# Two layers of local attention and gated feed-forward in one block instead of four, with the two sequences of a pair staggered

## The reference

```python
x = x + _layernorm(_L1_attn_ref(_layernorm(x, axis=-1), ...), axis=-1)
x = x + _layernorm(_L1_ffn_ref(_layernorm(x, axis=-1), L1_ffn_wqkv, ..., L1_ffn_w2, L1_ffn_b2), axis=-1)
x = x + _layernorm(_L2_attn_ref(_layernorm(x, axis=-1), ...), axis=-1)
```

```python
def _layer(x, wqkv, qs, ksc, wo, lg, lb, w1, b1, w2, b2):
    b, n, _ = x.shape
    h = shift_token(x)
    qkv = h @ wqkv
    q, k, v = jnp.split(qkv, 3, axis=-1)
    ...
    q = l2norm(q) * qs
    k = l2norm(k) * ksc
    q, k = rotary_xpos(q, k)
    o = local_attention(q, k, v)
    o = o.transpose(0, 2, 1, 3).reshape(b, n, INNER)
    x = x + o @ wo
    h = shift_token(x)
    mu = h.mean(-1, keepdims=True)
    var = h.var(-1, keepdims=True)
    h = (h - mu) / jnp.sqrt(var + 1e-05) * lg + lb
    h = h @ w1 + b1
    a, g = jnp.split(h, 2, axis=-1)
    h = a * jax.nn.gelu(g, approximate=False)
    x = x + h @ w2 + b2
    return x
```

## Time and profile before

| | us |
|---|---|
| median of three runs (3698.55 to 3700.59) | 3698.94 |
| span of the profiled execution, first to last instruction | 3714.3 |
| busy in it: PE, DVE, ACT, POOL | 2972.4, 2362.2, 1568.7, 773.5 |
| first call of `l1_ffn`: attention, layer 1 | 109.04 |
| feed-forward, layer 1 | 32.95 |
| attention, layer 2 | 106.73 |
| feed-forward, layer 2, and the stage's normalisation | 37.90 |

### The profile page before, as it was taken

The page is one execution under the profiler, slowest core; times in us unless marked ns, Lnnn a source line. Parts: engine busy times, 40 slices in busy tenths (PEclk is TensorE's granted clock), DMA queues, the critical chain, the costliest instruction groups (busy, mean ns, idle before and its releaser), DMA issues. The chain is left out here.

```text
span 3714.3 us, 89913 instructions
## 1 busy us (share of the span) xinstructions
PE 2972.4 (80%) x35888; PEld 2017.2 (54%) x35888; DVE 2362.2 (64%) x6687; ACT 1568.7 (42%) x3160; POOL 773.5 (21%) x823
## 2 busy tenths in 40 slices
PE   3768888689876788868986778876998688798996
PEld 2635556556554455556654445655655354475654
DVE  7575755665777466566677646646667776565457
ACT  4144534434344453534443544353444354344432
POOL 4121312121113121222111322132111122112101
PEclk8679999689987899969998889986999798999998
DMA  1011100000001100000000110000010101000000
GB/s 41 1 36 33 23 7 3 2 2 19 18 1 46 34 19 7 3 2 3 23 14 1 52 31 16 8 2 1 4 31 6 33 21 37 7 3 3 20 18 7
DMA packets 64209, 59.21 MB, mean 16 GB/s; under 512 B 16371, under 2 KB 53156, under 8 KB 63782
## 3 DMA queue, kind: packets, MB, share of 16 engines
q1 hardware_dynamic: 62550, 52.72, 5.2%
q10 hardware_dynamic: 1232, 0.61, 0.1%
HBM read 35.76 MB, written 2.10 MB: 10 GB/s over the span
## 5 line engine op out<-in xcount | busy, mean ns | idle before, releaser
L1333 POOL TENSOR_TENSOR l1t_ss<-l1t_ss,neghalf 128x16 f32<-128x16 f32 x48 | 182.4, 3799 | 333.2 <-DVE l1t_ss L1367 333.2
L256 ACT ACT_TABLE_LOAD x64 | 82.1, 1283 | 304.7 <-PEq L1677 106.5
L2260 ACT ACTIVATE l2r_P<-l2r_bank_score 128x512 f32<-128x512 f32 x240 | 130.3, 594 | 137.2 <-PE l2r_bank_score L1982 137.2
L2260 ACT ACTIVATE l2a_P<-l2a_bank_score 128x512 f32<-128x512 f32 x240 | 130.3, 594 | 131.5 <-PE l2a_bank_score L1982 131.5
L1544 PE MATMUL l1t_ring<-l1f_qkv,x_normT 128*128 128x512 f32 x288 | 162.5, 693 | 12.2 <-ACT x_normT L1238 12.2
L191 POOL TENSOR_TENSOR ln_y_rstd<-ln_var_eps,neghalf 128x4 f32<-128x4 f32 x52 | 52.8, 1015 | 546.5 <-DVE ln_var_eps L212 510.6
L2152 DVE CUSTOM_DVE_ANT_0 l2r_masked<-l2r_bank_ring,l2r_neg_wide 128x512 bf16<-128x512 f32 (+1 forms) x192 | 111.5, 622 | 57.5 <-PE l2r_bank_ring L1951 57.2
L2152 DVE CUSTOM_DVE_ANT_0 l2a_masked<-l2a_bank_ring,l2a_neg_wide 128x512 bf16<-128x512 f32 (+1 forms) x192 | 111.7, 622 | 56.0 <-PE l2a_bank_ring L1951 55.1
L1951 PE MATMUL l2r_bank_ring<-l2r_k_head,l2r_q_head 32*128 32x128 f32 x1824 | 131.6, 285 | 14.9 <-DVE l2r_m L2152 7.4
L1982 PE MATMUL l2a_bank_score<-l2a_q_head,l2a_k_head 32*128 32x128 f32 x1920 | 141.8, 285 | 1.8 <-DMA l2a_q_head<-l2a_shiftT 0.8
L1951 PE MATMUL l2a_bank_ring<-l2a_k_head,l2a_q_head 32*128 32x128 f32 x1824 | 133.1, 287 | 12.2 <-DVE l2a_m L2152 5.3
(11 more groups left out here) (1197 smaller groups left out, 8454.5 us busy)
## 6 DMA issues: line engine op xcount, KB each, us to landing
l1t_v_low<-l1t_v SPq DMA_DIRECT2D x84, 130.0 KB, 2.3
l2x_w<-in_L_ffn_w SPq DMA_DIRECT2D x72, 128.0 KB, 2.3
l1f_qkv<-in_L_ffn_wqkv SPq DMA_DIRECT2D x6, 768.0 KB, 4.3
l1t_v_low_last<-l1t_v_last SPq DMA_DIRECT2D x28, 130.0 KB, 2.3
l1f_tables<-in_l_tables SPq DMA_DIRECT2D x6, 512.0 KB, 5.7
l2e_w_last<-in_L_ffn_w SPq DMA_DIRECT2D x24, 128.0 KB, 2.2
x_in<-in_L_attn_hidden_states SPq DMA_DIRECT2D x8, 256.0 KB, 3.0
out<-x_res SPq DMA_DIRECT2D x8, 256.0 KB, 2.6
```

Of the source, the lines that this page charges most:

```text
L256: act.activation(b.warm[:, column:column + 1], b.neghalf[:, 0:1], func)
L1333: pool.tensor_tensor(ss[:, n % 2], ss[:, n % 2], b.neghalf[:, 0:2 * H8], ALU.pow).then_inc(s["rn_ready"], 1)
L2260: act.activation(self.P[:, use % self.P_RING].rearrange("k h q -> k (h q)"), self.score_bank(h, g)[:, :], ACT.Exp, scale=self.scale).then_ ...
```

## The change

The four blocks of a call become one, with one set of semaphores and one ring for everything.

- `TILE_ORDER` puts the first sequence's tiles ahead: (0,0), (1,0), (0,1), (2,0), (3,0), (1,1), (2,1), (3,1), written (tile, sequence). The first sequence's rows are complete after the fifth tile, the second's after the eighth.
- The parts of the feed-forward become functions of one sequence: `turn_rows`, `turn_shifted`, `turn_normed`, `up`, `down` on PE; `shifted_stats`, `shifted_norm`, `gate`, `add_rows` on DVE; `turned_rows`, `turned_normed`, `gate` on ACT. The streams are written out with these between the attention's last tiles and layer 2's first.
- The bias `b2` becomes row 85 of the third slice of `w2`, and row 85 of the third slice of `hid` holds ones; the product with a row of ones goes.
- Layer 2's tables, `qkv`, `wo` and feed-forward weights are loaded as soon as layer 1 has read its own, between the transfers of `v_low` in SP's stream.

```diff
-        for d in range(DEPTH):
-            before = l1_ffn_attention(nc, b, w, lw, d, before)
-            before = l1_ffn_mlp(nc, b, f, lw, d, before)
-    return before
...
+BIAS_CHUNK, BIAS_ROW = len(HID_ROWS) - 1, HID_ROWS[-1][1]
+HID_K = [rows + (i == BIAS_CHUNK) for i, (c, rows) in enumerate(HID_ROWS)]
+TILE_ORDER = [(0, 0), (1, 0), (0, 1), (2, 0), (3, 0), (1, 1), (2, 1), (3, 1)]
+TL = len(TILE_ORDER)
+LAST_FIRST = TILE_ORDER.index((NT - 1, 0))
```

SP's stream:

```diff
+            lw.load_tables(sync, 0, s["tab_in"])
+            lw.load_qkv(sync, 0, s["qkv_in"])
+            lw.load_wo(sync, 0, s["wo_in"])
+            lw.load_mlp(sync, 0, s["mlp_in"])
+            sync.wait_ge(s["tables_ready"], 1)
+            lw.load_tables(sync, 1, s["tab_in"])
+            for n, (d, j, p) in enumerate(tiles):
+                if n == TL:
+                    sync.wait_ge(s["v_psum"], TL)
+                    lw.load_qkv(sync, 1, s["qkv_in"])
+                    sync.wait_ge(s["tile_psum"], TL)
+                    lw.load_wo(sync, 1, s["wo_in"])
+                if n == TL + 2:
+                    sync.wait_ge(s["fy_psum"], PAIR)
+                    lw.load_mlp(sync, 1, s["mlp_in"])
                 sync.wait_ge(s["v_ready"], n + 1)
```

The last product, old and new, and the order of PE's stream (`a` is the feed-forward part, `n` the tile, `i` the tile's place in its layer):

```diff
-                    pe.matmul(out, b.ones[0:1, :], lw.b2[:], start=True, stop=False)
...
+                for j in range(NT):
+                    for i, rows in enumerate(HID_K):
+                        last = pe.matmul(bank[:, j * D:(j + 1) * D], hid[0:rows, p, i, j * 128:(j + 1) * 128],
+                                         lw.w2[0:rows, i, :], start=i == 0, stop=i == parts - 1)
+                last.then_inc(s["fy_psum"], 1)
...
+                    if i == LAST_FIRST + 2:
+                        turn_rows(a)
+                    values(n)
...
+                    if i == LAST_FIRST + 2:
+                        turn_shifted(a)
+                    if i + 1 < TL:
+                        turn_shift(n + 1)
+                n = here + TL - 1
+                turn_normed(a)
+                turn_output(n)
+                up(a, 0)
+                output(n)
+                up(a, 1)
+                turn_rows(a + 1)
+                up(a, 2)
+                turn_shifted(a + 1)
+                down(a)
+                turn_normed(a + 1)
...
+            tile_steps(0)
+            turn_x(2)
+            up(1, 0)
+            project(TL, "qk")
+            up(1, 1)
+            project(TL, "v")
+            up(1, 2)
+            project(TL + 1)
+            down(1)
+            turn_qk(TL)
+            turn_x(3)
+            maxima(TL)
+            project(TL + 2)
+            scores(TL)
+            turn_shift(TL)
+            tile_steps(TL)
+            for i in range(parts):
+                up(3, i)
+            down(3)
```

ACT's stream between the layers, and DVE's at the end of the call:

```diff
+            tile_steps(0)
+            warm(act, b, ACT.Gelu)
+            turned_normed(0)
+            turned_output(TL - 1)
+            gate(0, 0)
+            gate(0, 1)
+            turned_rows(1)
+            gate(0, 2)
+            turned_normed(1)
+            turned_x(2)
+            gate(1, 0)
+            copy_qk(TL)
+            gate(1, 1)
+            square_and_v(TL)
+            gate(1, 2)
+            copy_qk(TL + 1)
+            square_and_v(TL + 1)
+            warm(act, b, ACT.Exp, 1)
+            turned_qk(TL)
+            turned_x(3)
...
+            add_rows(2)
+            result_stats(0)
+            gate(3, 0)
+            gate(3, 1)
+            gate(3, 2)
+            dve.wait_ge(b.x_stored, 16 * PAIR)
+            result_add(0)
+            add_rows(3)
+            result_stats(1)
+            result_add(1)
```

More of the change, by code:

```diff
@@ L1282, in l1_ffn_attention @@
         place = {taker: i for i, taker in enumerate(takers)}
         def v_low_done(n):
[L1285 removed]
+            return sum(16 + 16 * (j > 0) for d, j, p in tiles[0:n + 1])
         def bank_of(what, n):
@@ L1538, in take, with turn_x, project @@
                 return bank_of(what, n)
-            def project(n, parts="qkv"):
-                j, p = tiles[n]
-                for what in parts:
+            def turn_x(r):
+                p, bank = r % PAIR, take("tx", r)
+                if r < PAIR:
+                    wait_xn(pe, s, p)
+                else:
+                    pe.wait_ge(s["fy_read"], r - PAIR + 1)
+                for j in range(NT):
+                    last = pe.transpose(bank[:, j * 128:(j + 1) * 128], b.xn[:, p, j, :], b.ident[:])
+                last.then_inc(s["tx_psum"], 1)
+            def project(n, what_parts="qkv"):
+                d, j, p = tiles[n]
+                pe.wait_ge(s["qkv_in"], 16 * (d + 1))
+                pe.wait_ge(s["tx_ready"], PAIR * d + p + 1)
+                for what in what_parts:
                     c = "qkv".index(what)
@@ new lines, in turn_shifted, with turn_normed @@
+            def turn_shifted(a):
+                bank = take("fh", a)
+                pe.wait_ge(s["fx_ready"], a + 1)
+                for j in range(NT):
+                    t = slice(j * 128, (j + 1) * 128)
+                    last = pe.transpose(bank[:, t], fT[:, a % PAIR, t], b.ident[:])
+                last.then_inc(s["fh_psum"], 1)
+            def turn_normed(a):
+                bank = take("fn", a)
+                pe.wait_ge(s["hn_ready"], a + 1)
+                for j in range(NT):
+                    last = pe.transpose(bank[:, j * 128:(j + 1) * 128], hn[:, a % PAIR, j, :], b.ident[:])
+                last.then_inc(s["fn_psum"], 1)
@@ L1643, in _ @@
+            busy(pe, b, s_bank[1], 10)
+            turn_x(0)
+            turn_x(1)
             project(0)
@@ L1792 @@
+        return [*s.values(), b.x_stored]
 H16 = 16
```

560 lines of the change are left out of this document (305 added, 255 removed).

## The result

The changed kernel takes 3570.32 us, the median of four runs (3559.92 to 3584.61), against 3698.74 for the kernel before (four runs here): a ratio of 0.965, 95% interval 0.9623 to 0.9676. The forecast was 3572 us, within 3540 to 3640, with a chance of 0.95 for faster. Run twice more beside the experiments, the change stood at 0.9635 (0.9609 to 0.966) and 0.9622 (0.96 to 0.9644).

A forecast was written before the change was run, and what follows sets the result against it. No engine was taken as full; waits between engines at the seams, 117 us of a call, bound it. Terms -22.6 - 10.1 + 2.2 - 1.2 = -31.7 a call, -127 us over four, from 3698.94 to 3572 us; range 3540 to 3640.

The forecast's parts named there:

- The seam between the layers: From layer 1's last subtract to layer 2's first: 48 us in place of 70.6, -22.6 a call, ends 42 and 54.
- I add 2 for stretches at the half clock: Allowance between the layers: 2 us on top of the followed chain of 45.9, giving 48.
- `down` of a sequence falls from 5.1 to 3.5: Feed-forward's last product on PE: without the bias product a sequence takes 3.5 us instead of 5.1.
- PE has 39 us of work: Between the layers: PE's work at the full clock is 39 us, so it is neither idle for long nor the bound.
- The seam at the call's end: From layer 2's last subtract to the next stage: 36.5 us in place of 46.6, -10.1 a call, ends 33 and 40.
- The seventh tile: Inside each layer: eight transposes moved there on PE add 1.1 us, twice a call, +2.2, ends 1 and 4.
- The call's start: First projection waits for the first sequence's shifted copy alone: -1.2 us a call, ends -1.2 and 0.
- The sum: Whole program: -31.7 us a call, -127 over four calls, set against the runs' median 3698.94, giving 3572 us.
- Half of it is lost to strict order in the queues: Rival, in the seams: rounds of `up`, Gelu and `gate` run one after another; -16.4 a call, 3633 us; chance 0.20.
- PE becomes the bound: Rival: queues cross better than followed and the seams end at PE's work; -48 us a call, 3506 us; chance 0.08.
- The clock stays at half: Rival, in the new seams: PE's work runs at half clock, a call is 17 us longer, 3767 us; chance 0.04.
- The table loads: ACT between the layers: 1.28 us each from the trace, ending at 3.7 and 35.2, before first use; no cost.

The follow-up runs named there:

- the experiment with the later rows: The changed kernel with the first sequence's turned rows and shifted copies one tile later, beside the eighth tile: 3610.21 us, ratio 0.9757 to the kernel before.
- the spare products: The changed kernel with layer 2's tables scaled later and extra products in PE's idle time: 3557.01 us, run again 3561.45 us; the change beside it 3567.26 and 3557.57.

## Why the prediction was right

*The seam between the layers* was followed on the queues, and the end of the chain came out within 1.3 us of the trace, the entries before it within 1.1. The term was -25.6 instead of -22.6 a call: 1.3 of the difference is the chain, the rest "I add 2 for stretches at the half clock", as there were none in three of four seams. "`down` of a sequence falls from 5.1 to 3.5" was mis-sized: it takes 2.7 to 2.9, because a one-row product also slows the products behind it; here it lies beside DVE's chain, and the sum did not feel it. "PE has 39 us of work" is 36.8 at the full clock.

*The seam at the call's end*: 36.5 forecast, 36.2 measured; without the allowance 35.3 against 35.0 in the call whose clock stayed up, and 1.6 more in the others. Here `down` is on the chain and 0.6 shorter than its 3.5 (465.85 to 468.80); small errors the other way hide half of that. *The seventh tile*: +1.1 forecast, +0.88 measured, twice a call. *The call's start*: -1.2 in the first call (9.95 to 8.74 us from the stage before to the first projection), but only -0.5 on average over four, near the other end of its range, 0.

*The sum.* The four calls, from the stage before to the stage behind, fell from 1178.3 to 1032.7 us in the profiles, -36.4 a call where -31.7 was forecast; everything else in the program is 0.7 us apart. With the other profiles of the two kernels (1171.8 before; 1032.2 and 1034.8 after) the calls fall by 34 to 37 us each. By the medians the whole is -128 in the first comparison, and -139 and -143 in the two others. So the forecast was some 10 to 20 us short, most of it the 3 us a call of the seam between the layers, and that 3572 lies within 2 us of 3570.32 is luck of the first comparison. That the sum was set against the median, 15.4 us below the span, was right: the second profile of the kernel before spans 3696.2.

*The rivals.* "Half of it is lost to strict order in the queues": the second `gate` of the second sequence waited 0.4 us for `rotate` (Gelu ends at 350.28, `gate` starts at 350.67) and the third 0.6 for the sum of squares, as the forecast had counted; the three rounds did not become a chain of their own. "PE becomes the bound": PE is idle for 7.8 us of 44.6, and the experiment with the later rows shows that the waits set the seam. "The clock stays at half": 1.00, 1.00, 0.96 and 1.00 between the layers. With the one-row product put back it fell to half there for 6.8 to 10.2 us of three seams, well short of the six tenths of the work that this rival needs; but the bias row, which I had costed by its instructions alone, is part of what kept it away. The rival's reading that the clock fell "whenever PE had done little, 6.30 us of 10.24" does not hold: that share was read inside the stretch at half clock, and with the one-row product such a stretch has 6.80 of 6.82.

*The table loads.* Both loads between the layers take 1.28 us, ending at 3.3 and 34.6 after the last subtract, ahead of what needs them:

```profile
325.23 1.28 ACT L256 ACT_TABLE_LOAD   x1
356.50 1.28 ACT L256 ACT_TABLE_LOAD   x1
357.79 0.20 ACT L256 ACTIVATE act_warm<-neghalf 128x1 f32<-128x1 f32 x1
```

The Trainium skill, "ScalarE: Activation LUTs", section "What ACT_TABLE_LOAD costs", has 2.66 us for a switch, a load of 1.28 and a drain of 1.38. The load agrees; but the next instruction on ACT starts at 357.79, 0.01 us after the load's end at 357.78, so no drain is seen and the measurement decides for 1.28. By the page's figure the prediction's two loads would end at 5.1 and 36.6, not at its 4.8 and 36.4; nothing in its sum hangs on that.

What the prediction did not ask is which part gives the gain; there my later theory was wrong in its size, and the table above stands in its place.

## What to carry to other kernels

Where no engine is full for tens of microseconds between two parts of a program, follow each step on the queues with durations from the trace: the wait that ends last decides, and here such a sum was good to 1.3 us in 45. Splitting the work so that one half's chain runs beneath the other's dense part gave about half the gain, and joining four blocks into one, with earlier loads, most of the rest. Price a removed product by the period of its group with and without it, not by its own record, and compare seams by profiles but totals by runs. Before you believe a few microseconds of a total, count the stretches at the half clock on both sides.

## What the runs showed that I had not expected

- An f32 product of one row by 128 columns costs 0.58 us in its group (1.25 against 0.67 for 128 tokens), one of 128 rows 0.23 (0.90). The Trainium skill, "TensorE: Matmul & The Clock Gate", section "Why this matters for your kernels", says that a product of 32 rows takes the same time as one of 128. For 32 rows, which other stages of this kernel have, the trace agrees (in the change a record of L2160 has 0.270 us in the median, one of `down` 0.275), and for 85 and 86 rows too; for one row, of which the page says nothing, it does not hold.
- The granted clock fell to 0.50 for 6.82 us in which PE was busy for 6.80, with one-row products among its work, and stayed at 1.00 at the same place with products of 128 rows. The same is seen without one-row products at the end of the change's first call (457.24 to 460.65, PE busy throughout, clock 0.50). So an engine that shows no idle time is not always one at the full clock; at the half clock the same work also fills more of the time.
- Time taken out of the seams came back in part in the tiles, at the same work and a lower clock: 11 to 16 us with the bias row alone, 5 with the spare products. In both it is more tile periods with a stretch at the half clock (13 against 6 and 3; 10 against 7). What brings these stretches is not shown.
- Stages that no edit touches summed to 2536.0 us in one profile of the kernel before and 2524.5 in another, and to 2522 to 2548 over all 14 profiles.
